# A graph network kernel whose gathers carry their milestone waits themselves

## The chip, the cores and the metric

The kernel runs on one core of a Trainium2 chip. The metric is the device time of one execution in microseconds (us). Three executions of the kernel before took 4169.53, 4178.44 and 4180.32 us; their median, 4178.44 us, is the time that the change is set against. On this core each engine has its own stream of instructions and waits for others by semaphores: TensorE (PE; its weight loads are listed as PEld), VectorE (DVE), ScalarE (ACT), GpSimd (POOL) and SyncE (SP). POOL issues nothing here but indirect DMAs, the gathers.

## What is computed

Two graph layers over 12500 nodes of 48 features and 200000 edges, sorted by destination. The first layer sends each edge's two nodes and its 32 attributes through a small network; the second adds the source node's row to 48 edge attributes. Both sum the messages by destination, add a residual and normalise each node.

```python
# layer 0
tmp = jnp.concatenate([x[dst], x[src], edge_attr_32], axis=1)
msg = jax.nn.relu(tmp @ W1 + b1) @ W2 + b2
x = _layernorm(x + segment_sum(msg, dst), axis=-1)
# layer 1
m = jax.nn.relu(x[src] + edge_attr_48)
x = _layernorm(x + (1.0 + eps[0]) * x + segment_sum(m, dst), axis=-1)
```

## The kernel before

The edges are cut into 391 groups of 512 edges, each group into four tiles of 128 edges. `x[src]` is brought by gathers: one indirect DMA (line 597 to 598, issued by the helper at line 561) fetches 128 rows of 48 floats for one tile into `edge[:, g % RING, t, 48:96]`, a ring of `RING` = 8 groups. For some groups (`PICK0_OF` in layer 0, `PICK_OF` in layer 1) the fourth tile is not gathered but picked: PE multiplies one-hot matrices `at_place` with all rows kept in `x1_parts` (`pick_rows`, line 880), DVE selects the row out of the product (lines 1104, 1113, 1118). So a group has three or four gathers.

Layer 0 runs by pairs of groups, in steps p. PE in step p (`steps0`, line 811) transposes the gathered tiles of pair p (line 805; it waits for the gathers of each group first, line 801), makes the windows of the pair (line 824, counted by the semaphore `awin`), sums the messages of pair p-3 (line 779), does the output layer of pair p-2 (line 787, counted by `msgp`) and the hidden layer of pair p-1 (line 838, counted by `pre`), then the products of the picks (line 880, a third of a step's products counted by `third`). ACT copies and activates, DVE makes one-hots, splits messages (line 1035 in layer 0, line 1037 in layer 1) and accumulates (line 1028). Layer 1 runs by single groups: DVE adds the gathered rows to the edge attributes (line 1137; it waits for the gathers first), ACT applies the relu (line 707), PE sums (line 779) and makes products (line 880).

POOL walks through the gathers in order of their groups. What it waits for is in three places:

- `gathers` (line 588) waits once per group until the group eight before it has been read (`trans` in layer 0, `sum` in layer 1), so that its place in the ring is free.
- `in_step` (line 570) spreads the up to eight gathers of a pair over PE's step: the first waits for `awin` of step g//2 - 2, the second for `msgp`, the third and fourth for `pre`, the fifth to seventh for the thirds of the products; the eighth waits for nothing.
- `in_thirds` (line 582) does so in layer 1 with the thirds of one group's products, for the first three gathers of a group.

A wait written ahead of an instruction is carried by that instruction. Each gather has a semaphore increment ahead of it, `pool.sem_inc(s_passed, 1)` (line 597), and this is the instruction that carries the waits. Nobody waits for `s_passed`. The path of the general layers (line 616), with increments of its own, is not run with these inputs.

SP's load of `x_win` for step p (line 476) waits for `awin` of step p - 2 (line 474): the same milestone for which the first gather of pair p waits.

Of the kernel before, what the change touches and what calls it, by code (L numbers as in the profile page):

```python
# [106 lines left out]
def thirds_of(products):  # L107

    n = len(products)
    return [n * k // 3 - 1 for k in (1, 2, 3)] if n >= 3 else []  # L110
# [30 lines left out]
def build(nc, x, xT, src_tiles, dst_tiles, dst_groups, e32, e48, w1, w2, b1, b2, eps, ident, iota, center, normed,  # L141
          src_rows, src_columns, places, earlier, spare, out):
    ctx = ExitStack()
    with ctx:
# [6 lines left out]
        def sem(name):  # L151
            return ctx.enter_context(nc.semaphore(name))
# [115 lines left out]
        s_passed = sem("s_passed")  # L268
# [46 lines left out]
        def wait_count(eng, s, h, per, n):  # L315
            if isinstance(h, int) and per * h + n <= 0:
                return
            eng.wait_ge(s, h * per + n)

        def peeled(eng, body, count):  # L320
            body(0)
            with eng.Fori(1, count) as i:
                body(i)
# [22 lines left out]
        def wait_for(eng, s, g):  # L346

            if g >= 0:
                eng.wait_ge(s, g + 1)
# [14 lines left out]
        def gathered(S, g):  # L364

            return TILES - 1 if g in (PICK_OF if S is S1 else PICK0_OF) else TILES
# [9 lines left out]
        def groups_of(i):  # L376
            return range(LAST + 1 if last_iteration(i) else UNROLL)
# [17 lines left out]
        def by_width(eng, general, windowed):  # L395

            eng.wait_ge(s_known, 2)
            wide_groups = eng.value_load(n_wide_i[0:1, 0:1], min_val=0, max_val=SLOTS)
            with eng.If(wide_groups > 0):
                general()  # L400
            with eng.Else():
                windowed()
# [155 lines left out]
        @block.gpsimd  # L558
        def _(pool):
            def gather(cols, rows_of, index, done):  # L560
                pool.indirect_dma_start(out=cols, out_offset=None, in_=rows_of,  # L561
                                        in_offset=bass.IndirectOffsetOnAxis(ap=index, axis=0)).then_inc(done, 16)

            def src_of(i, u, t):
                return src_all[:, (i * UNROLL + u) * TILES + t:(i * UNROLL + u) * TILES + t + 1]

            def thirds_before(products, step):
                return sum(len(thirds_of(u)) for s, u in products.items() if 0 <= s < step)

            def in_step(g, k):  # L570

                p = g // 2 - 2
                if k == 0:
                    wait_for(pool, S0["awin"], p)
                elif k == 1:
                    wait_for(pool, S0["msgp"], 2 * p - 4)
                elif k < 4:
                    wait_for(pool, S0["pre"], 2 * p - 4 + k)
                elif k < 7 and p >= 0 and thirds_of(PRODUCTS0.get(p, ())):
                    pool.wait_ge(S0["third"], thirds_before(PRODUCTS0, p) + k - 3)  # L580

            def in_thirds(g, t):

                step = g - 4
                if step >= 0 and t < 3 and thirds_of(PRODUCTS.get(step, ())):
                    pool.wait_ge(S1["third"], thirds_before(PRODUCTS, step) + t + 1)

            def gathers(S, rows_of, read, i):
                for u in groups_of(i):
                    g = i * UNROLL + u  # L590
                    wait_for(pool, S[read], g - RING)
                    for t in range(gathered(S, g)):
                        if S is S0:
                            in_step(g, g % 2 * TILES + t)
                        else:
                            in_thirds(g, t)
                        pool.sem_inc(s_passed, 1)
                        gather(edge[:, g % RING, t, D:2 * D], rows_of, src_of(i, u, t), S["rows"][g % RING])


            pool.wait_ge(s_first_src, 16)
            gathers(S0, x, "trans", 0)

            def windowed():
                def others(S, rows_of, read):
                    for i in range(1, ITERS):
                        if S is S0 and i == FIRST:
                            pool.wait_ge(s_src, 16)
                        gathers(S, rows_of, read, i)

                others(S0, x, "trans")
                pool.wait_ge(s_x1, 16 * CHUNKS)
                gathers(S1, x1_dram, "sum", 0)
                others(S1, x1_dram, "sum")

            def general_layer(G, n):
                def steps(h):
                    for u in range(2):


                        pool.wait_ge(G["idx"], h * 16 + 16)
                        wait_count(pool, G["dst"], h, 2, u + 1)
                        pool.sem_inc(s_passed, 1)
                        for t in range(TILES):
                            gather(edge[:, u, t, D:2 * D], x1_dram if n else x, idx[:, u, t:t + 1], G["rows"])
                            if n == 0:
                                gather(edge[:, u, t, 0:D], x, dst_idx[:, t:t + 1], G["rows"])
                        for t in range(TILES):


                            wait_count(pool, G["addend"], h, 2 * TILES, u * TILES + t + 1)
                            pool.sem_inc(s_passed, 1)
                            pool.indirect_dma_start(out=table[n], in_=addend[:, :], in_offset=None, compute_op=ALU.add,
                                                    out_offset=bass.IndirectOffsetOnAxis(ap=target[:, :], axis=0),
                                                    ).then_inc(G["added"], 16)

                pool.wait_ge(G["table"], 16)
                peeled(pool, steps, HALVES)

            def general():  # L640
                for u in range(UNROLL):
                    pool.wait_ge(S0["rows"][u], 16 * TILES)
                general_layer(G0, 0)
                pool.wait_ge(s_x1, 16 * CHUNKS)
                general_layer(G1, 1)

            by_width(pool, general, windowed)
# [712 lines left out]
```

## Time and profile before

| | |
|---|---|
| median of 3 runs | 4178.44 us (4169.53 to 4180.32) |
| profiled execution, its own time | 4175.66 us |
| its span, first to last instruction | 4173.9 us |
| PE busy | 3670.4 us (88%) |
| POOL busy | 2628.5 us (63%), nearly all of it in 2688 gathers |
| DVE busy | 2370.4 us (57%) |
| ACT busy | 750.7 us (18%) |
| mean granted TensorE clock | 0.883 of full speed |

The profile lists each engine's instructions with start and duration; idle time in front of one is put down to what ended it ("issue" where nothing shown ended it, "remote" where the semaphore's source could not be told). Semaphore increments, waits, register and branch instructions are not listed and do not count as busy, so POOL's `sem_inc` shows only as idle time between gathers. A gather's duration on POOL is the time in which it writes the transfer's descriptors, not that in which the data move. PE's ends are modelled. Layer 0 lasts until about 2210 us, layer 1 begins at about 2250 us.

### The profile page before, as it was taken

Reading aid. Unit: us, or ns where it says so; the run is one execution under the profiler, and the core shown is the slowest. Engines: PE = TensorE matmul, PEld = TensorE weight load, DVE = VectorE, ACT = ScalarE, POOL = GpSimd, SP = SyncE. Lnnn points to the kernel's source line nnn. Section 1 sums busy time; section 2 is a strip of 40 time slices with the busy share of each in tenths; the row PEclk is TensorE's granted clock in tenths of the full one; section 3 lists DMA queues with packets and bytes.
Section 4 is the critical chain, followed back from the end, with each engine's and each line's share of the span. In section 5 each row is a group of like instructions: output and inputs, shape, how many; then the busy total and the mean of one; then the engine's idle time right before and its main releaser. Section 6 shows DMA issues by size and latency. Waiting matters only on the chain.

```text
span 4173.9 us, 54004 instructions
## 1 busy us (share of the span) xinstructions
PE 3670.4 (88%) x18202; PEld 3023.8 (72%) x18202; DVE 2370.4 (57%) x5096; ACT 750.7 (18%) x1666; POOL 2628.5 (63%) x2692
## 2 busy tenths in 40 slices
PE   4798898888898998899998888888888889888998
PEld 3576677677777777777786777777777777777876
DVE  3344444444444444444546777776777677776766
ACT  1222222222222222222331000000000000001111
POOL 6666666666666666666664666666666666666664
PEclk7688889889898898889998899999899999998887
DMA  5222222222222222222221222222222222222221
GB/s 103 33 34 35 34 34 36 34 34 36 34 35 35 34 35 35 34 34 40 38 37 41 46 49 48 49 49 46 48 48 49 46 49 48 49 48 48 51 52 43
DMA packets 408253, 178.47 MB, mean 43 GB/s; under 512 B 279196, under 2 KB 407138, under 8 KB 407874
## 3 DMA queue, kind: packets, MB, share of 16 engines
q0 software_dynamic: 86016, 66.23, 11.6%
q1 hardware_dynamic: 319778, 108.26, 11.3%
q8 instruction: 146, 2.39, 0.2%
q14 instruction: 135, 1.11, 0.1%
q10 hardware_dynamic: 2178, 0.48, 0.1%
HBM read 169.74 MB, written 5.00 MB: 42 GB/s over the span
## 4 chain that ended last, share of the span: by engine, by line
PE 18%; DVE 17%; issue 12%; another core or an unknown queue 10%; ACT 1%; DVEq 0%; DMA 0%; POOL 0%; POOLq 0%
PE ps_h L880 5%; DVE at_place L1104 5%; DVE picked L1113 5%; PE ps_t L880 4%; PE ps_early L880 2%; PE ps_as L779 2%; DVE edgeT L1137 2%; PE ps_out L787 1%; PE ps_h L838 1%; DVE msg L1037 1%; PE ps_nodes L890 1%; ACT msg L707 1%; DVE hot L1014 1%; DVE acc L1028 1%
## 5 line engine op out<-in xcount | busy, mean ns | idle before, releaser
L561 POOL DMA_INDIRECT edge<-x,resid_sb x1430 | 1421.7, 994 | 789.1 <-issue 404.9
L561 POOL DMA_INDIRECT edge<-x_dram,resid_sb x1258 | 1206.6, 959 | 731.0 <-issue 394.8
L880 PE MATMUL ps_h<-x_parts,at_place 125*128 125x480 f32 x3080 | 799.8, 416 | 33.2 <-issue 27.3
L1104 DVE TENSOR_TENSOR at_place<-place_row,ps_out 125x1280 fp32r<-125x1280 f32 x440 | 651.4, 1481 | 236.1 <-ACT msg L687 180.6
L880 PE MATMUL ps_t<-x_parts,at_place 125*128 125x480 f32 x3040 | 757.2, 404 | 20.4 <-issue 20.1
L880 PE MATMUL ps_early<-x_parts,at_place 125*128 125x480 f32 x2680 | 733.7, 423 | 31.4 <-DVE edge L1014 18.2
L880 PEld LDWEIGHTS ps_h<-x_parts,at_place 125*128 125x128 f32 x3080 | 640.6, 211 | 150.9 <-issue 43.4
L880 PEld LDWEIGHTS ps_early<-x_parts,at_place 125*128 125x128 f32 x2680 | 526.1, 198 | 230.8 <-issue 130.5
L880 PEld LDWEIGHTS ps_t<-x_parts,at_place 125*128 125x128 f32 x3040 | 602.2, 201 | 123.1 <-issue 30.2
L779 PE MATMUL ps_as<-hot,msg 128*97 128x48 f32 x3128 | 376.4, 254 | 244.8 <-DVE msg L1037 120.6
L779 PEld LDWEIGHTS ps_as<-hot,msg 128*97 128x97 f32 x3128 | 359.3, 181 | 287.8 <-DVE msg L1037 118.6
L838 PE MATMUL ps_h<-edgeT,w_edge 128*128 128x512 f32 x782 | 488.4, 757 | 18.3 <-DMA edge<-e 14.4
L787 PE MATMUL ps_out<-w_sb,hT 128*128 128x48 f32 x3128 | 474.0, 311 | 31.0 <-issue 27.7
L787 PEld LDWEIGHTS ps_out<-w_sb,hT 128*128 128x128 f32 x3128 | 452.1, 228 | 30.3 <-issue 26.6
L1057 DVE COPY w_edge<-ps_as 48x128 f32<-48x128 f32 x391 | 112.3, 287 | 602.7 <-remote 458.4
L707 ACT ACTIVATE msg<-edgeT 128x192 fp32r<-128x192 f32 x391 | 142.6, 365 | 1566.9 <-DVE edgeT L1137 912.9
L1028 DVE TENSOR_TENSOR acc<-acc,ps_as 97x48 f32 x782 | 159.8, 204 | 443.7 <-remote 337.3
L805 PE MATMUL ps_t<-ident_sb,edge 128*128 128x128 f32 x1564 | 228.0, 286 | 99.3 <-DMA edge<-x,resid_sb 66.9
L683 ACT ACTIVATE edgeT<-ps_t 128x512 f32<-128x512 f32 x391 | 219.8, 601 | 482.5 <-PE ps_t L805 206.6
L805 PEld LDWEIGHTS ps_t<-ident_sb,edge 128*128 128x128 f32 x1564 | 194.4, 149 | 142.9 <-DMA edge<-x,resid_sb 76.1
L1118 DVE TENSOR_REDUCE edge<-picked 128x48 f32<-128x480 f32 x440 | 287.4, 653 | 15.1
L1113 DVE SCALAR_TENSOR_TENSOR picked<-iota_sb,col_rest,ps_early 128x480 f32<-128x480 f32 x134 | 143.9, 1074 | 261.2 <-remote 112.8
(77 smaller groups left out, 2140.5 us busy)
## 6 DMA issues: line engine op xcount, KB each, us to landing
edgeT<-e SPq DMA_DIRECT2D x196, 192.0 KB
place_row<-rows_dram SPq DMA_DIRECT2D x440, 62.5 KB
edge<-e SPq DMA_DIRECT2D x196, 128.0 KB
edge<-x,resid_sb POOLq DMA_INDIRECT x1430
edge<-x_dram,resid_sb POOLq DMA_INDIRECT x1258
x_win<-xT SPq DMA_DIRECT2D x391, 9.0 KB
acc<-xT SPq DMA_DIRECT2D x10, 234.4 KB
feats<-x SPq DMA_DIRECT2D x10, 234.4 KB
```

Source lines behind the costliest of these rows:

```text
L561: pool.indirect_dma_start(out=cols, out_offset=None, in_=rows_of, in_offset=bass.IndirectOffsetOnAxis(ap=index, axis=0)).then_inc(done, 16)
L683: nc.scalar.activation(edgeT[:, g % UNROLL, :], ps_t[g % 2][:, :], ACT.Copy).then_inc(S0["edgeT"], 1)
L707: nc.scalar.activation(msg[:, u, :, 0:D], pre1[:, u, :, :], ACT.Relu).then_inc(S1["high"], 1)
L779: last = nc.tensor.matmul(ps_s[g % 2], lhsT=msg[:, g % UNROLL, t, 0:SUMS], rhs=hot[:, g % UNROLL, t, :], start=(t == 0), stop=(t == TILES ...
L787: last = nc.tensor.matmul(ps_m[:, g % 2, t, :], lhsT=hT[:, g % 2, t * P:(t + 1) * P], rhs=w2_sb[:, :], start=True, stop=True)
L805: last = nc.tensor.transpose(ps_t[g % 2][:, t * P:(t + 1) * P], edge[:, g % RING, t, :], ident_sb[:, :])
L838: nc.tensor.matmul(ps_h[g % 2][:, :], lhsT=w_edge[:, g % UNROLL, :], rhs=edgeT[:, g % UNROLL, :], start=True, stop=True).then_inc(S0["pre" ...
L880: last = nc.tensor.matmul(banks[q % len(banks)], lhsT=at_place[:, q % PLACED, c, :], rhs=x1_parts[:, c, part, :], start=(c == 0 and part = ...
L1028: nc.vector.tensor_tensor(acc[0:SUMS, bass.ds(first, WIN)], acc[0:SUMS, bass.ds(first, WIN)], ps_s[g % 2], ALU.add).then_inc(S["acc"], 1)
L1104: nc.vector.tensor_tensor(at_place[:, q % PLACED, :, :], place_row[:, q % PLACED, :].unsqueeze(1).to_broadcast([NP, CHUNKS, P]), ps_places ...
L1113: nc.vector.scalar_tensor_tensor(picked[:, :, :].rearrange("p f k -> p k f"), iota_sb[:, 0:CB].unsqueeze(2).to_broadcast([P, CB, D]), col_ ...
L1118: nc.vector.tensor_reduce(edge[:, group % RING, TILES - 1, D:2 * D], picked[:, :, :], AX.X, ALU.add).then_inc(S["picked"], 1)
```

## The change

The increment ahead of each gather in `gathers` is removed. The waits are unchanged, and now stand directly ahead of the gather. The other increments of `s_passed` stay.

```diff
                         if S is S0:
                             in_step(g, g % 2 * TILES + t)
                         else:
                             in_thirds(g, t)
-                        pool.sem_inc(s_passed, 1)
                         gather(edge[:, g % RING, t, D:2 * D], rows_of, src_of(i, u, t), S["rows"][g % RING])
```

## Rows read from the trace of the kernel before

**Rows 1.** The page: busy time of each engine, and the granted clock in 40 slices

```profile
PE 3670.4 (88%) x18202; PEld 3023.8 (72%) x18202; DVE 2370.4 (57%) x5096; ACT 750.7 (18%) x1666; POOL 2628.5 (63%) x2692
...
PEclk7688889889898898889998899999899999998887
```

**Rows 2.** Busy time by stage: stretch, length, then PE, PEld, DVE, ACT, POOL, clock, DMA

```profile
1000.00:1400.00 400.00, 359.59 (x1912) 287.58 (x1909) 182.67 (x446) 104.98 (x221) 257.35 (x261) 0.89 0.22 35
...
3000.00:3400.00 400.00, 359.16 (x1672) 305.26 (x1671) 289.39 (x530) 30.34 (x83) 254.32 (x266) 0.91 0.23 48
```

**Rows 3.** Groups of instructions: line, engine, shapes, count, busy us, mean ns, idle before

```profile
L561 POOL DMA_INDIRECT edge<-x,resid_sb x1430 | 1421.7, 994 | 789.1 <-issue 404.9 <-remote 261.6 <-PE ps_h L838 56.1
L561 POOL DMA_INDIRECT edge<-x_dram,resid_sb x1258 | 1206.6, 959 | 731.0 <-issue 394.8 <-PE ps_h L880 138.6 <-PE ps_t L880 97.4
...
L1137 DVE TENSOR_TENSOR edgeT<-edge,edgeT 128x192 f32<-128x192 f32 x391 | 138.4, 354 | 1.2 <-DMA edge<-x_dram,resid_sb 1.0
...
L1014 DVE TENSOR_TENSOR hot<-iota_sb,rel 128x192 fp32r<-128x192 f32 x391 | 121.4, 352 | 0.0
```

**Rows 4.** Timeline of POOL, first gathers: start us, us, then idle before and releaser

```profile
5.21 0.95 POOL L561 DMA_INDIRECT edge<-x,resid_sb  x1 [0.31 <-issue]
6.46 0.95 POOL L561 DMA_INDIRECT edge<-x,resid_sb  x1 [0.30 <-issue]
```

**Rows 5.** Timeline, three places where `awin` releases SP's load and a gather

```profile
407.28 0.79 SPq L476 DMA_DIRECT2D x_win<-xT  x2
...
407.94 0.95 POOL L561 DMA_INDIRECT edge<-x,resid_sb  x1 [1.99 <-remote]
...
899.14 0.80 SPq L476 DMA_DIRECT2D x_win<-xT  x2
...
899.80 0.94 POOL L561 DMA_INDIRECT edge<-x,resid_sb  x1 [2.35 <-remote]
...
1022.24 0.80 SPq L476 DMA_DIRECT2D x_win<-xT  x2
...
1022.90 0.94 POOL L561 DMA_INDIRECT edge<-x,resid_sb  x1 [2.49 <-PE ps_out L787]
```

**Rows 6.** Who waited for whom, whole span: us in total, times, longest us

```profile
POOL edge L561 <- issue: 799.6, 2234, 35.4
...
PE ps_as L779 <- DVE msg L1037: 120.6, 61, 4.0
...
PEld ps_t L805 <- DMA edge<-x,resid_sb: 76.1, 38, 4.5
...
PE ps_t L805 <- DMA edge<-x,resid_sb: 66.9, 35, 4.2
PE ps_as L779 <- DVE msg L1035: 63.3, 34, 4.2
```

**Rows 7.** Line 561: who waited for the gathers in layer 1 (us, times)

```profile
  DVE edgeT L1137: 1.0, 1
```

**Rows 8.** Timeline of PE behind two waits for a gather

```profile
911.73 0.66 PE L805 MATMUL ps_t<-ident_sb,edge 128*128 128x128 f32 x4 [2.17 <-DMA edge<-x,resid_sb]
...
916.85 1.50 PE L779 MATMUL ps_as<-hot,msg 128*97 128x48 f32 x8 [4.24 <-DVE msg L1035]
...
1179.83 0.66 PE L805 MATMUL ps_t<-ident_sb,edge 128*128 128x128 f32 x4 [3.30 <-DMA edge<-x,resid_sb]
...
1180.49 1.53 PE L779 MATMUL ps_as<-hot,msg 128*97 128x48 f32 x8
```

**Rows 9.** PE around the first of these waits: stretch, length, busy, clock, DMA

```profile
900.00:908.00 8.00, 8.00 (x52) 1.00 0.41 63
...
914.00:924.00 10.00, 7.15 (x27) 0.51 0.24 37
924.00:930.00 6.00, 6.00 (x30) 0.96 0.11 16
```

## The prediction

> **What bounds the kernel now.** I read the page's busy times first. PE is at work for 88% of the span and POOL for 63% [rows 1], so PE is the engine that the time hangs on, and POOL matters only where it makes PE wait. The table by stage says the same of the middle of each layer: in 400 us of layer 0 PE is busy 359.6 us, in 400 us of layer 1 359.2 us, at a granted clock of about 0.9 [rows 2].
>
> Next, how near POOL is to its own limit. Where nothing is waited for, a gather takes 0.95 us and the next begins 0.30 us behind it: 1.25 us from start to start [rows 4]. In the middle of layer 0 POOL does 261 gathers in 400 us, one per 1.53 us; in layer 1 266, one per 1.50 us [rows 2]. So POOL would get by with some 82% of the time. Its idle time, 789.1 + 731.0 = 1520 us, is 2688 x 0.30 = 806 us of these steps between neighbours and 714 us of real waiting [rows 3].
>
> Last, who waits for the gathers. In layer 0 PE's transposes do: 76.1 us in 38 waits by the weight loads' count, 66.9 us in 35 by the matmuls' [rows 6]. In layer 1 the only reader is DVE's addition, and it waited 1.0 us in all [rows 7]. Whatever the change does to a gather by less than a microsecond is therefore worth at most those 76 us, and nothing in layer 1. The other waits of PE are for DVE's messages, 120.6 us in layer 1 and 63.3 us in layer 0 [rows 6].
>
> **What the change removes: the increments.** 2688 of them. Do they cost POOL time when it is busy? Their only room is the 0.30 us between neighbours. The row of the first gathers shows 0.30 with an increment and no wait ahead of each, and no row shows two gathers without an increment between them, so the trace bounds the part of the increment by 0 and 0.30 us. I take 0: each gather's 0.95 us would cover an increment issued ahead of time, while the one before is still writing descriptors. If I am wrong by the whole 0.30, POOL gains 2688 x 0.30 = 806 us, of which PE can use only what it waits for gathers, 76 us at the very most.
>
> **What it moves: the wait, from the increment to the gather.** This matters where POOL stands idle until the milestone comes. The trace shows such handoffs beside a second engine that waits for the same count of `awin`: SP's load of `x_win` began at 407.28, 899.14 and 1022.24 us, the gather at 407.94, 899.80 and 1022.90 us, each time 0.66 us later [rows 5]. So a gather starts at least 0.66 us behind its milestone, and a load that carries the same wait itself goes at once. If the change made the gather as quick as the load, each such handoff would be 0.66 us shorter; if the work of handing the gather to POOL starts only behind the wait, whoever carries it, it is 0. I take the upper end less a little, 0.5 us, since the engine that carries its own wait is the nearest row, and a gather surely has something left to do.
>
> The Trainium skill ("Perfetto Trace Analysis", section "DMA Instruction — SWDGE (GPSIMD)") draws it so: the sequencer decodes such a DMA, pushes it into a wait queue, is free for the next one, and the semaphore is waited for in that queue. By that rule the decoding of the gather would lie ahead of the milestone; an increment as carrier keeps it behind. The 0.66 us agree with the second half; that a gather with a wait is quicker no run here shows yet.
>
> What becomes of 0.5 us? The gathers behind the first follow at 1.25 us, so the whole chain up to the next stop moves by it, and a late group lands 0.5 us earlier. There are 38 waits, mean 2.0 us, so nearly all have 0.5 us to give: 38 x 0.5 = 19 us. Not all of it stays. Behind the wait that ended at 911.73 us PE stood still again, 4.24 us, for DVE's messages; had the transposes begun 0.5 us earlier, that second wait would have been 0.5 us longer. Behind the one that ended at 1179.83 us PE ran on without a gap, and there the gain stays [rows 8]. PE's 34 waits for line 1035 against 35 for gathers [rows 6] say that the two kinds are about equally frequent, so I keep half: **about 10 us**. In layer 1 DVE gets its rows early enough already: 0 us. Its cover is the slack that the 1.0 us show; if that is gone, a gather that comes earlier still costs nothing.
>
> Two waits on one gather (the ring's and the first milestone of a group): one of the two may need a carrier of its own, as now. It is the ring's that is old news, eight groups back, so I cost it at nothing; if the carrier held the milestone instead, the first gather of a pair would keep its 0.66 us, and the second to seventh would gain.
>
> Nothing is queued on POOL but gathers, so behind a waiting gather stand only later gathers, and they stood behind the increment before. SP and the other queues are not touched. Ring and milestones are the same counts, so no gather can start before the event that it waited for.
>
> The sum against the profiled execution: 4175.66 - 10 = 4165.7 us. That execution lies 2.8 us under the median of the runs, so **4168 us** on the scale of the median 4178.44. The case's own range is from no gain to all 19 us and the lower end of the cost, 38 x 0.66 = 25 us: 4153 to 4179.
>
> **Rivals.**
>
> Rival 1, *the handoff stays as it is*: the gather is prepared only when its wait is over. For it: nothing in the trace shows a gather that carries a wait. Against it: SP's 0.66 us lead. It gives 4178 us. The Trainium skill has a page that speaks for this one ("Vector Engine (DVE) Microarchitecture Reference", section "Instruction fetch and dispatch (NX sequencer)"): the sequencer's loop issues the semaphore wait before it reads the opcode. If issuing meant sitting it out, the change would move nothing; the page tells of DVE, not POOL.
>
> Rival 2, on the other side, *a carried wait lengthens the step between gathers*: POOL can no longer line up the next gather while one is at work, and each carrying gather costs x more than 1.25 us. Its place is the late groups of layer 0: up to eight gathers in a row end just before PE wants them, seven of them carrying a wait, so each of the 38 waits grows by 7x. It decides from the point where 7x is over the 0.5 us of the handoff, x = 0.07 us. At x = 0.15 the 38 waits are 38 x (1.05 - 0.5) = 21 us longer if no group is added to the late ones; with as many more groups falling late, 42 us: 4199 to 4220 us. The far end is x = 0.66, the whole handoff paid every time: 1.91 us for a gather where one is due every 1.53 us [rows 2], and POOL would bound the kernel: 2688 x 1.91 = 5134 us. Against it: on DVE an addition that carries a wait takes 354 ns, a comparison of the same size that carries none 352 [rows 3], so an engine does not pay for a carried wait in busy time; for POOL no row says so.
>
> Rival 3, *the clock multiplies the gain*. Ahead of the wait that ended at 911.73 us PE ran without a gap at a granted clock of 1.00, the full 2.4 GHz; then it stood idle for 2.17 and 4.24 us, and the next 10 us were granted 0.51, near the lower level of 1.2 GHz, before it was back at 0.96 [rows 8, 9]. Ten microseconds at half speed lose some 5 us of PE's work. If the shorter idle times spare a quarter of the 38 late groups this fall, 9 x 5 = 45 us come on top of 10: about 4125 us. Against it: 0.5 us off a stop of 6 us in all is little. The same coupling can turn round (one fall more), which blurs every case by some 5 to 10 us.
>
> **How the numbers follow.** Forecast, handoff shorter and half kept: 0.40, 4168 us. Rival 1: 0.25, 4178 us. Rival 2: 0.20, mostly 4199 to 4220, with a tail. Rival 3: 0.15, 4125 us. A measurement of this kernel can tell about 0.3%, 12.5 us, from no change: under 4165.9 us is faster, over 4191.0 slower. The forecast's range lies on both sides of 4165.9; I give 0.14 of its 0.40 to faster and the rest to the same. Rival 1 gives 0.22 to the same, and 0.03 to slower for the blur. Rival 2 is slower, Rival 3 faster. Faster 0.29, same 0.48, slower 0.23. The range has to hold 8 in 10: I cut the lower half of Rival 3 and the tail of Rival 2, which gives 4132 to 4218 us.
>
> **What would show it.** The handoff: at places where SP's load of line 476 and a gather are released together, the gather's start should be 0.1 to 0.2 us behind SP's instead of 0.66 (0.66 again under Rival 1). The increment's cost: neighbours still at 1.25 us; 1.0 would say that it did cost something, 1.3 or more is Rival 2. The wait of line 805 for gathers should fall from 76 to below 60 us, and the wait of line 779 for line 1035 rise by some of it. Rival 3 shows as a mean clock above 0.89. Layer 1 should keep its length within a few microseconds; if it moves by more, the gathers act on PE or DVE by a way that no wait shows, and my whole accounting by waits is wrong.

## The result, and the profile after

The changed kernel takes 4103.34 us in the median of four runs (4102.24 to 4104.37), the kernel before 4177.16 (4169.53 to 4180.32). The ratio is 0.9823, with a 95% interval of 0.9811 to 0.9835: 73.8 us faster, where 10 were forecast and the range ended at 4132. All line numbers behind 597 are one less in the changed kernel: line 805 is now 804, 779 is 778, 1137 is 1136.

The page of the kernel after: its span, the busy time of each engine and the granted clock in 40 slices. They answer to [rows 1].

```profile
span 4100.4 us, 52068 instructions
...
PE 3620.0 (88%) x18202; PEld 2975.9 (73%) x18202; DVE 2372.4 (58%) x5096; ACT 751.3 (18%) x1666; POOL 2626.6 (64%) x2692
...
PEclk7789899899898998898998989999999999999988
```

The span is 73.5 us shorter. PE has the same 18202 matmuls and is busy 50.4 us less with them (3670.4 before), its idle time is 23.1 us less; the mean granted clock rose from 0.883 to 0.898. In this pair of traces two thirds of the gain show up as faster matmuls, one third as less standing still; further down two traces of one chip split it the other way. POOL is busy as long as before.

Next the groups of the gathers (idle time before them and what ended it, as in [rows 3]) and where they begin and end (durations in ns, then first and last start in us), for the kernel after, and then the same beginnings and ends for the kernel before:

```profile
L561 POOL DMA_INDIRECT edge<-x,resid_sb x1430 | 1421.5, 994 | 747.5 <-issue 375.7 <-remote 244.0 <-PE ps_early L879 62.3
L561 POOL DMA_INDIRECT edge<-x_dram,resid_sb x1258 | 1204.9, 958 | 703.2 <-issue 347.3 <-PE ps_h L879 154.8 <-PE ps_t L879 107.3
...
L561 POOL DMA_INDIRECT edge<-x,resid_sb x1430: 938/944/1997, 3.1 to 2168.5; - x179
L561 POOL DMA_INDIRECT edge<-x_dram,resid_sb x1258: 938/944/1442, 2204.3 to 4076.6; - x180
```

```profile
L561 POOL DMA_INDIRECT edge<-x,resid_sb x1430: 941/947/2005, 3.8 to 2210.2; - x179
L561 POOL DMA_INDIRECT edge<-x_dram,resid_sb x1258: 941/947/1466, 2246.7 to 4148.0; - x180
```

Layer 0 ends 41.7 us earlier. The gathers of layer 1 take 1872.3 us from first to last instead of 1901.3: 29.0 us less in a layer in which, by [rows 7], nobody waits for them. POOL's idle time fell from 1520.1 to 1450.7 us. With its work fixed that is only the shorter span over again, so it shows where the time went on POOL and not why.

Two tables by stage, columns as in [rows 2]: layer 0 without its start, and layer 1, for the kernel after and then for the kernel before.

```profile
50.00:2168.50 2118.50, 1898.72 (x10110) 1515.76 (x10111) 952.97 (x2417) 569.89 (x1191) 1388.58 (x1396) 0.88 0.23 38
...
2204.30:4076.60 1872.30, 1662.62 (x7818) 1410.45 (x7817) 1357.59 (x2532) 161.19 (x432) 1203.98 (x1257) 0.93 0.24 49
```

```profile
50.00:2210.00 2160.00, 1921.37 (x10110) 1535.68 (x10111) 951.21 (x2416) 567.89 (x1190) 1389.25 (x1397) 0.87 0.23 37
2247.00:4148.00 1901.00, 1687.90 (x7808) 1436.55 (x7807) 1354.91 (x2526) 161.36 (x431) 1205.41 (x1258) 0.90 0.23 48
```

In layer 1 PE is busy 25.3 us less at a clock of 0.93 instead of 0.90; that is nearly the whole of its gain. In layer 0 22.7 us are busy time and 18.9 idle time (2160.00 - 1921.37 = 238.6 before, 219.8 after).

The waits of the kernel after that answer to [rows 6] (us in total, times, longest), then PE's waits ahead of its sums in layer 1 alone, for the kernel before and the one after:

```profile
PE ps_as L778 <- DVE msg L1036: 101.3, 54, 4.3
...
PE ps_t L804 <- DMA edge<-x,resid_sb: 30.9, 22, 3.7
...
PE ps_as L778 <- DVE msg L1034: 26.6, 15, 4.2
```

```profile
PE ps_as L779 <- DVE msg L1037: 115.4, 59, 4.0
PE ps_as L779 <- issue: 44.5, 46, 3.6
```

```profile
PE ps_as L778 <- DVE msg L1036: 98.5, 53, 4.3
PE ps_as L778 <- issue: 60.9, 48, 3.6
```

PE's wait for gathers fell from 66.9 us, that for layer 0's messages from 63.3. That for layer 1's messages fell from 120.6 only by name: ahead of the same sums PE also stood still where no listed event ended it ("issue"), and there the time rose by as much. With both names and 1.7 and 1.8 us for an accumulation PE stood 161.6 us ahead of layer 1's sums before and 161.2 after. In this pair the gain of layer 1 is therefore not in these waits, but in PE's busy time at a higher clock.

Last, the handoff itself. ACT's activation of line 692 (691 after) waits for the same count of `pre` as the third or fourth gather of a pair, and like SP it carries its wait itself, so places where both stood idle show how far the gather is behind. Timeline of the kernel before, then of the kernel after:

```profile
645.32 1.27 ACT L692 ACTIVATE hT<-ps_h,b_sb 128x512 f32<-128x512 f32 x2 [0.16 <-remote]
...
646.09 0.94 POOL L561 DMA_INDIRECT edge<-x,resid_sb  x1 [2.93 <-remote]
```

```profile
1911.56 1.26 ACT L691 ACTIVATE hT<-ps_h,b_sb 128x512 f32<-128x512 f32 x2 [0.84 <-remote]
...
1911.79 0.94 POOL L561 DMA_INDIRECT edge<-x,resid_sb  x1 [1.48 <-PE ps_early L879]
```

The distance is 0.77 us before and 0.23 after; it is 0.77 or 0.78 in all thirteen such places of the one trace and 0.23 or 0.24 in all five of the other. So a gather with one wait starts 0.54 us sooner. The first gather of a pair, which has the ring's wait as well as a milestone, does not. In the kernel after, SP and such a gather at a milestone of `awin`:

```profile
334.79 0.80 SPq L476 DMA_DIRECT2D x_win<-xT  x2
...
335.41 0.94 POOL L561 DMA_INDIRECT edge<-x,resid_sb  x1 [2.50 <-remote]
```

0.62 us, where [rows 5] had 0.66. Of two waits ahead of one instruction the one written first stays on it, and the later one, here the milestone, gets a carrier of its own.

### The profile page after: what moved, and what is told of

It reads as the page before. It is cut to its first block, busy times and chain, and to the rows that moved or that the text cites. A ratio compares the mean times of both kernels' runs of the same rounds, so it can differ in the third digit from the quotient of the medians.

```text
span 4100.4 us, 52068 instructions
## 1 busy us (share of the span) xinstructions
PE 3620.0 (88%) x18202; PEld 2975.9 (73%) x18202; DVE 2372.4 (58%) x5096; ACT 751.3 (18%) x1666; POOL 2626.6 (64%) x2692
## 4 chain that ended last, share of the span: by engine, by line
PE 32%; DVE 22%; issue 20%; another core or an unknown queue 17%; POOL 3%; ACT 2%; DMA 1%; DVEq 1%; SPq 0%; POOLq 0%
PE ps_early L879 8%; DVE at_place L1103 6%; DVE picked L1112 6%; PE ps_h L837 5%; PE ps_out L786 5%; PE ps_h L879 3%; POOL edge L561 3%; PE ps_as L778 3%; PE ps_t L879 3%; PE ps_t L804 3%; DVE edgeT L1136 2%; DVE hot L1013 2%; DVE acc L1027 1%; DVE msg L1036 1%
## 5 line engine op out<-in xcount | busy, mean ns | idle before, releaser
L879 PE MATMUL ps_early<-x_parts,at_place 125*128 125x480 f32 x2680 | 745.7, 426 | 68.3 <-DVE edge L1013 38.0
L879 PE MATMUL ps_h<-x_parts,at_place 125*128 125x480 f32 x3080 | 775.1, 407 | 25.2 <-issue 19.6
L879 PEld LDWEIGHTS ps_h<-x_parts,at_place 125*128 125x128 f32 x3080 | 621.8, 205 | 136.7 <-issue 34.3
L837 PE MATMUL ps_h<-edgeT,w_edge 128*128 128x512 f32 x782 | 473.6, 735 | 20.4 <-DMA edge<-e 13.9
L786 PE MATMUL ps_out<-w_sb,hT 128*128 128x48 f32 x3128 | 454.0, 302 | 24.9 <-issue 24.4
L786 PEld LDWEIGHTS ps_out<-w_sb,hT 128*128 128x128 f32 x3128 | 431.6, 219 | 27.6 <-issue 27.3
L686 ACT ACTIVATE msg<-ps_out 128x192 fp32r<-128x192 f32 x391 | 108.1, 328 | 914.3 <-remote 797.6
```

Source lines behind the costliest of these rows:

```text
L786: last = nc.tensor.matmul(ps_m[:, g % 2, t, :], lhsT=hT[:, g % 2, t * P:(t + 1) * P], rhs=w2_sb[:, :], start=True, stop=True)
L837: nc.tensor.matmul(ps_h[g % 2][:, :], lhsT=w_edge[:, g % UNROLL, :], rhs=edgeT[:, g % UNROLL, :], start=True, stop=True).then_inc(S0["pre" ...
L879: last = nc.tensor.matmul(banks[q % len(banks)], lhsT=at_place[:, q % PLACED, c, :], rhs=x1_parts[:, c, part, :], start=(c == 0 and part = ...
```

## The experiments

Every ratio is to the kernel before on the same chip, with its 95% interval; chips differ by 1%, so the times themselves compare only within a group. The letters of the theories stand for this. I: the 2688 increments themselves are what costs. H: what counts is how far a gather starts behind its milestone (the handoff). P: what counts is the way in which POOL's sequencer waits, not the distance. L: PE's semaphore updates reach the other engines late while POOL works through gathers, and that closes a loop of POOL and PE. Q and D, inside L: it is the gathers that are queued that hold the updates, or it is the length of POOL's pauses that lets them out. Many edits are counted in *stops*, places in which POOL stood idle for over 0.35 us. By the starts of the gathers the kernel before has 425: 172 in layer 0 and 122 in layer 1 at gathers with one wait, 131 at gathers with two (the first of each group).

### Is it the handoff or the increments, and in which layer?

**The increments kept, but ahead of the waits.** The gather carries the wait, and all 2688 increments are still issued.

```diff
-                    wait_for(pool, S[read], g - RING)
                     for t in range(gathered(S, g)):
+                        pool.sem_inc(s_passed, 1)
+                        if t == 0:
+                            wait_for(pool, S[read], g - RING)
                         ...
-                        pool.sem_inc(s_passed, 1)
                         gather(...)
```

> All 2688 increments are kept, but each stands ahead of the waits, so the gather carries its wait itself as in the changed kernel. Theory H (handoff: a gather that carries its wait starts sooner behind its milestone): the increments as such cost nothing, so about 4103 us, within 10 us. Theory I (increments: 2688 fewer semaphore updates leave room for PE's): the gain is gone, about 4177 us.

Measured: 4070.10 us against 4134.06, ratio 0.9838 (0.9822 to 0.9855). The ratio is that of the change within the intervals, with every increment in place: one increment a gather costs nothing that shows, its place does.

**No increments, but a carrier for the milestone.** A wait that has long been met is written ahead of the milestone, so that it stays on the gather and the milestone gets a carrier of its own.

```diff
                     for t in range(gathered(S, g)):
+                        if t > 0:
+                            pool.wait_ge(s_first_src, 16)
                         ...
-                        pool.sem_inc(s_passed, 1)
```

> No increments, but the second to fourth gather of a group get a second wait, ahead of the milestone's, on a semaphore that reached its value at the start; of two waits the later one stays on an instruction of its own ahead of the gather, so every milestone has a carrier again, only without an increment. Theory H: as the kernel before, 4165 to 4180 us, and the gathers start about 0.65 us behind SP's load again. Theory I: as the changed kernel, about 4103 us.

Measured: 4124.10 us, ratio 0.9979 (0.9964 to 0.9994). Without increments, but with the old handoff, nearly all of the gain is gone. Its timeline shows nearly the old distance, 0.74 or 0.75 us in 22 of 23 places:

```profile
847.32 1.27 ACT L693 ACTIVATE hT<-ps_h,b_sb 128x512 f32<-128x512 f32 x2 [0.84 <-remote]
...
848.06 0.95 POOL L561 DMA_INDIRECT edge<-x,resid_sb  x1 [1.72 <-remote]
```

**The change in one layer alone.** The increments stay in the other layer.

```diff
-                        pool.sem_inc(s_passed, 1)
+                        if S is S1:              # layer 0 changed; S0 here: layer 1 changed
+                            pool.sem_inc(s_passed, 1)
```

> The change in layer 0 alone. In the changed kernel the last gather of layer 0 came 42 us earlier and layer 1 took 29 us less. If each layer gains by itself: 4177 - 42 = 4135 us, with layer 1 as long as before (1901 us from first to last gather). If layer 1's gain comes from somewhere ahead of it: about 4106 us.

> The change in layer 1 alone, where nobody waited for a gather. If the 29 us of layer 1 are the change's own: 4177 - 29 = 4148 us, with a granted clock in layer 1 of 0.93 for 0.90. If they are an accident of how the layers meet: within 10 us of 4177.

Measured: layer 0 alone 4083.26 us, ratio 0.9879 (0.9862 to 0.9895), 51 us; layer 1 alone 4112.81 us, 0.9946 (0.9929 to 0.9962), 21 us. Their sum is the whole gain. Layer 1 gains by itself: it is not a gift of a layer 0 that ended in better order. The two ran on one chip, so their traces compare directly. Layer 1 from its first gather to its last, columns as in [rows 2], first with layer 0 changed, then with layer 1 changed:

```profile
2176.00:4055.00 1879.00, 1665.37 (x7817) 1421.66 (x7815) 1356.28 (x2530) 160.85 (x431) 1202.77 (x1258) 0.92 0.25 49
```

```profile
2231.00:4089.00 1858.00, 1658.35 (x7816) 1413.38 (x7815) 1355.50 (x2527) 160.81 (x431) 1200.21 (x1257) 0.92 0.25 49
```

Where layer 1 is changed it is 21 us shorter, by 7 us of PE's busy time and 14 us of its idle time. In the kernel before neither PE nor, but for 1.0 us, DVE waits for a gather in it, so the gain comes by a way on which no wait for a gather lies.

### The size of the handoff as a dose

**The kernel before once more, as a profile for its chip,** beside the next one.

> The kernel before, for a trace on the chip of the next three. No theory is at stake; time within 0.3% of the runs of before beside it.

Measured, in one execution: 4137.29 us, POOL's idle time 781.3 + 712.7 us.

**The ring's wait behind the milestone.** The milestone is written first and stays on the gather also where there are two waits.

```diff
-                    wait_for(pool, S[read], g - RING)
                     for t in range(gathered(S, g)):
                         ...
-                        pool.sem_inc(s_passed, 1)
+                        if t == 0:
+                            wait_for(pool, S[read], g - RING)
                         gather(...)
```

> The changed kernel with the two waits of a group's first gather in the other order, milestone first and ring second, so that this gather carries its milestone too and the ring's wait gets the carrier. In the changed kernel the first gathers of pairs still started 0.63 us behind SP's load. Theory H: now 0.1 to 0.25 us, and as about a third of POOL's stops are at first gathers, another 10 to 25 us: ratio to before 0.976 to 0.980. Theory P (what costs is POOL's sequencer standing in a wait ahead of the gathers, which holds up PE's updates, not the later start) says the same; if neither, ratio 0.982.

Measured: 4031.29 us (4028.75 to 4036.32) against 4136.57, ratio 0.9758 (0.9738 to 0.9777), mean clock 0.911. It beats both kernels, by 0.65% more than the change did. Its timeline at a milestone of `awin`; then PE's waits ahead of its sums behind 2150 us, in the kernel before on this chip and in this one:

```profile
1028.12 0.80 SPq L476 DMA_DIRECT2D x_win<-xT  x2
...
1028.25 0.94 POOL L561 DMA_INDIRECT edge<-x,resid_sb  x1 [1.59 <-remote]
```

```profile
PE ps_as L779 <- DVE msg L1037: 113.1, 53, 4.1
PE ps_as L779 <- issue: 62.7, 67, 4.1
```

```profile
PE ps_as L779 <- issue: 122.3, 61, 3.5
PE ps_as L779 <- DVE msg L1037: 23.7, 29, 3.5
```

The gather of a pair's start is now 0.13 us behind SP. PE stands still ahead of layer 1's sums for 146 us instead of 176; the fall from 113.1 to 23.7 by itself is mostly a change of name, since "issue" doubled. Both theories had foretold the gain, so the run does not choose between H and P.

**Seven increments in place of one,** behind the waits, so that a gather starts later behind its milestone while the step between neighbours stays at 1.25 us.

```diff
-                        pool.sem_inc(s_passed, 1)
+                        for _ in range(7):
+                            pool.sem_inc(s_passed, 1)
```

> The kernel before with seven increments ahead of each gather for one. Twelve of them made POOL itself slower (1.43 us from gather to gather, for 1.25), which mixes two causes; seven should leave the 1.25 us, and draw out only the handoff, by 6 x 0.07 = 0.4 us (0.07 us each from the twelve: 1.43 = 0.55 + 12 x 0.07). Theory H: the change took off some 0.6 us and gained 1.77%, so 0.4 us more should lose about 1.2%: ratio 1.008 to 1.016. Theory P: 0.997 to 1.003.

Measured: 4306.43 us against 4176.35, ratio 1.0315 (1.0292 to 1.0337). The direction is that of H; the size is two to four times what I expected. Timeline: the distance to ACT, and two neighbours.

```profile
808.60 1.44 ACT L693 ACTIVATE hT<-ps_h,b_sb 128x512 f32<-128x512 f32 x2 [0.20 <-remote]
...
809.85 0.94 POOL L561 DMA_INDIRECT edge<-x,resid_sb  x1 [1.08 <-remote]
```

```profile
34.08 0.95 POOL L561 DMA_INDIRECT edge<-x,resid_sb  x1 [0.30 <-issue]
35.33 0.94 POOL L561 DMA_INDIRECT edge<-x,resid_sb  x1 [0.30 <-issue]
```

The distance grew by 0.48 us, from 0.77 to 1.25, for six more increments: 0.08 us each. But that is not all that these increments did. The trace lists each of them too: most take 0.02 us, but 1009 of the 18816 take over 0.2 us, up to 1.39 us, and 145 us of this lie in POOL's pauses. POOL stood idle for over 0.35 us 636 times instead of 425, 42 times in front of a gather that waits for nothing. With one increment a gather none took over 0.2 us. So part of the 130 us is increments that were themselves held up, and this run alone does not rule out P. Here gathers also come late for both readers: DVE waited for them 292.1 us in layer 1 (1.0 before), PE 124.8 us in layer 0 (66.9 before).

The doses, side by side. *Stops* are those of the kernel before whose handoff the edit changes; *at most* is their number by the change.

| edit | handoff | stops | at most | measured | kept |
|---|---|---|---|---|---|
| the change | 0.77 to 0.23 us | 294 | -159 us | -73.8 us | 46% |
| layer 0 alone | the same | 172 | -93 us | -51 us | 55% |
| layer 1 alone | the same | 122 | -66 us | -21 us | 32% |
| ring's wait moved, on top of the change | 0.66 to 0.13 us | 131 | -69 us | -27 us | 39% |
| seven increments (not the handoff alone) | 0.77 to 1.25 us | 425 | +204 us | +130 us | 64% |

Where the handoff was shortened the time follows it at POOL's own stops, with a third to somewhat over half kept. That it does so when the handoff is lengthened is shown in direction only.

**Twelve increments, behind the waits or ahead of them.**

```diff
-                        pool.sem_inc(s_passed, 1)
+                        for _ in range(12):      # or the same lines ahead of the waits
+                            pool.sem_inc(s_passed, 1)
```

> The kernel before with twelve increments ahead of each gather for one, the first of them carrying the waits: the handoff is drawn out by eleven increments, an estimated 0.3 to 0.6 us. Theory H: slower than before, by as much again as the change gained for each 0.5 us: ratio 1.01 to 1.02. Theory P: as before, ratio 0.997 to 1.003.

> Twelve increments per gather as in the run with twelve, but ahead of the waits, so that the gather carries its wait: POOL as slow (1.43 us per gather), the handoff short. Theory H: better than the 1.058 of that run by at least the change's 1.8%, 1.01 to 1.04. If only POOL's rate counts: 1.058 again.

Measured: behind the waits 4370.36 us, ratio 1.0578 (1.0557 to 1.0600); ahead of them 4463.99 us, ratio 1.0697 (1.0668 to 1.0727). Both were misses: at most 1.02 was expected of the first, 1.01 to 1.04 of the second. H had the second 1.8% ahead of the first, and it came out 1.1% behind; why, these runs don't show. Neither tells what it was made for, since both changed the rate of POOL as well, and in both some 700 increments took over 0.2 us. Timeline of the first:

```profile
33.40 0.94 POOL L561 DMA_INDIRECT edge<-x,resid_sb  x1 [0.48 <-issue]
34.82 0.94 POOL L561 DMA_INDIRECT edge<-x,resid_sb  x1 [0.47 <-issue]
```

The step is 1.42 us instead of 1.25: POOL's sequencer has become slower than the gathers. 12 x 0.08 leave 0.46 us for the gather itself, about the 0.54 us by which the handoff shrank, so the handoff that went is most likely the sequencer's own work on the gather, which now lies ahead of the milestone. In the kernel before the increments that nothing held follow each other at 0.55 to 0.57 us, which is the same sum: one increment and one gather. At 1.42 us a gather POOL is short of time (one is due every 1.53 us in layer 0, [rows 2]), and DVE waits 521.5 us for gathers.

### Why layer 1 moves

**Layer 1 without milestones.** Its gathers wait for their place in the ring alone and so run ahead as far as they can.

```diff
                         if S is S0:
                             in_step(g, g % 2 * TILES + t)
-                        else:
-                            in_thirds(g, t)
-                        pool.sem_inc(s_passed, 1)
```

> The changed kernel with layer 1's milestones left out: its gathers wait only for their place in the ring. If an early gather is what layer 1 gains by: layer 1 shorter still, ratio 0.965 to 0.98. If the milestones are needed, to keep gathers from other work: layer 1 longer, ratio 0.985 to 1.01. If the gather's time means nothing there: 0.982.

Measured: 4292.04 us against 4136.57, ratio 1.0391 (1.0369 to 1.0413); its layer 1 takes 2076.7 us instead of 1876.6. The largest loss expected was 1.01, so this was a miss as well. Gathers that are earlier are not better as such. Where DVE stood idle for a sum, it started in the median 8.0 us after PE's sum had ended, where that was 3.4 us in the kernel before.

**Layer 1 without gathers.** The changed kernel; layer 1 computes on rows left in the ring.

```diff
-                gathers(S1, x1_dram, "sum", 0)
-                others(S1, x1_dram, "sum")
                 ...
-                    dve.wait_ge(S1["rows"][g % RING], landed(S1, g))
```

> The changed kernel without the gathers of layer 1, and without DVE's wait for them: layer 1 computes on whatever rows its ring holds. It asks why a gather that nobody waits for can cost layer 1 time. Theory L: PE's semaphore updates reach the other engines late while POOL works through gathers in a row; so without gathers DVE's accumulations no longer start microseconds behind PE's sums (in the kernel before: median 3.4 us where DVE had been idle), and layer 1 falls from 1877 us by 100 us or more: ratio under 0.96. Otherwise the lateness is PE's own, and layer 1 keeps its length: ratio 0.975 to 0.985.

Measured: 3759.25 us against 4176.35, ratio 0.9012 (0.8995 to 0.9029), the changed layer 0 included. From PE's first sum of layer 1 to its last it is 1530 us, where the changed kernel, on another chip, takes 1869. The table by stage, 400 us of its layer 1:

```profile
2800.00:3200.00 400.00, 400.00 (x2070) 348.74 (x2069) 360.18 (x663) 37.51 (x103) 0.00 (x0) 1.00 0.14 39
```

In these 400 us PE never stands still and is granted the full clock. Now the same pair of instructions in both kernels, DVE's accumulation behind PE's sum: first the kernel before, between them POOL's gathers, then the kernel without gathers in layer 1.

```profile
3031.93 0.79 PE L779 MATMUL ps_as<-hot,msg 128*97 128x48 f32 x8
...
3036.37 0.95 POOL L561 DMA_INDIRECT edge<-x_dram,resid_sb  x1 [0.30 <-issue]
...
3039.60 0.54 DVE L1028 TENSOR_TENSOR acc<-acc,ps_as 97x48 f32 x2 [5.82 <-remote]
...
3040.22 1.00 POOL L561 DMA_INDIRECT edge<-x_dram,resid_sb  x1 [2.91 <-PE ps_t L880]
...
3040.32 1.05 DVE L1113 SCALAR_TENSOR_TENSOR picked<-iota_sb,col_rest,ps_h 128x480 f32<-128x480 f32 x1
...
3040.55 0.49 PE L779 MATMUL ps_as<-hot,msg 128*97 128x48 f32 x4 [0.65 <-DVE msg L1037]
```

```profile
3009.21 0.79 PE L776 MATMUL ps_as<-hot,msg 128*97 128x48 f32 x8
...
3010.20 0.54 DVE L1025 TENSOR_TENSOR acc<-acc,ps_as 97x48 f32 x2 [1.29 <-PE ps_as L776]
```

Without gathers DVE starts 0.20 us after PE's last sum (3009.21 + 0.79 = 3010.00, then 3010.20), and so in 87 of the 89 such places of layer 1 (0.55 and 1.83 us in the other two). Before, it starts 6.9 us after it (3031.93 + 0.79 = 3032.72, then 3039.60), having stood idle for 5.82 us; POOL had been through a row of gathers that ended at 3037.32, and it too was let go by PE only now, 0.62 us behind DVE. The next instruction of PE then waited 0.65 us for DVE's message. PE's sum had long been done; what came late was the word of it. The waits of DVE for these sums between 2400 and 3600 us, the kernel before and then the one without gathers:

```profile
DVE acc L1028 <- remote: 206.0, 45, 8.8
```

```profile
DVE acc L1025 <- PE ps_as L776: 70.4, 67, 3.7
```

The trace also records the updates of the semaphores with their times, which the views above don't print; some are missing where gathers run (328 of 391 are there for layer 1's sums before, all 391 without gathers). In the example the updates of the two sums stand at 3036.58 and 3039.41 us, 4.2 and 6.7 us behind the ends of the sums. Right behind them seven updates of PE's products follow from 3039.46 to 3039.85 us, at most 0.1 us apart, though PE ends such products up to 1.3 us apart. So it is not PE that was late, but its updates, which were held and came out in a row. Without gathers every update of layer 1's sums stands 0.01 us behind the end of its sum. In the kernel before 52% of them stand over 1 us behind one; of DVE's recorded updates it is 3 of 1995, of ACT's 1 of 945.

So L holds in its first half: PE's updates are late only where gathers are at work. Whether that is how gathers act on PE without anybody waiting for them, the second half, fits all that was seen but is inferred.

The same share, of the recorded updates of layer 1's sums that stand over 1 us behind the latest end of a sum before them (a lower bound of the lateness), for the kernels of this document:

| kernel | recorded | over 1 us |
|---|---|---|
| before | 328 | 52% |
| the change | 343 | 66% |
| ring's wait moved | 329 | 61% |
| ring's wait moved, with the memset below | 340 | 80% |
| ring's wait moved, ten increments ahead, below | 293 | 19% |
| twelve increments, behind the waits / ahead | 238 / 221 | 4% / 7% |
| no gathers in layer 1 | 391 | 0% |

This also speaks against P: in the kernels in which gathers carry their waits PE's updates are not held less, but rather more often. The change does not cure the lateness; it takes 0.54 us off what is added to it.

**Is it the queue of gathers or the lack of a pause?** Two kernels, both on top of the one with the ring's wait moved. The first slows POOL's sequencer by ten increments ahead of the waits, so that fewer gathers stand ready in the queue. The second puts a short memset between the gathers of layer 1.

```diff
                     for t in range(gathered(S, g)):
+                        for _ in range(10):
+                            pool.sem_inc(s_passed, 1)
```

```diff
+                        if S is S1:
+                            nc.gpsimd.memset(pause[:, g * TILES + t:g * TILES + t + 1], 0)
```

> The kernel with swapped waits plus ten increments ahead of the waits of each gather. With 0.55 + 10 x 0.073 = 1.28 us per gather POOL's sequencer becomes as slow as POOL's gathers (1.25), so that hardly any gather stands queued behind another, while the pause between two stays about 0.33 us. Theory Q (queued gathers hold PE's updates): the late accumulations of layer 1 are gone, though the time may rise with POOL's rate. Theory D (the pause is too short): they stay late, median 3 to 4 us, as in the kernel with swapped waits. On the time: ratio 0.98 to 1.02 either way.

> The kernel with swapped waits, and in layer 1 a memset of one byte per partition on POOL ahead of each gather's waits: other work between gathers that can stay queued. Theory D: the longer time from gather to gather lets PE's updates out, and the late accumulations of layer 1 are gone, as in the runs with twelve increments. Theory Q: they stay late, median 3 us or more. Layer 1 is some 5% longer if POOL's rate falls to 1.4 us per gather.

Measured: ten increments 4435.75 us against 4163.97, ratio 1.0651 (1.0624 to 1.0678), a miss on the time (0.98 to 1.02 were expected); the memset 4075.99 us, 0.9786 (0.9770 to 0.9803). With ten increments DVE stood idle for only 10 accumulations in layer 1, and those were as late as ever (2.3 to 6.3 us, median 3.54): it now waited 528.1 us for gathers, so the engines stood at other places than before. DVE's waits therefore don't tell whether updates were still held. The recorded updates do: 19% of them over 1 us late instead of 61%. In layer 0 ACT's copy of messages started in the median 0.29 us behind PE's output layer instead of 3.18 us in the kernel with the ring's wait moved. The pause between neighbours was hardly longer: in layer 1 it was 0.30 or 0.31 us for 587 of 1257 gathers and at most 0.38 for 827. Fewer gathers queued, nearly the same pause, fewer late updates: that is what Q foretold. The memset fitted into the 0.30 us between neighbours, and the median lateness stayed at 4.07 us: other work between queued gathers doesn't let the updates out. It did not lengthen the pause, so D was not put to the test by itself; the evidence leans to Q, and a limit on the number of queued gathers by their landing was not tried. Of the miss on the time one part shows: 1056 of the increments took over 0.2 us, 163 us of it in POOL's pauses.

## Why the prediction was wrong, point by point

**The handoff: right.** A gather that carries its milestone starts 0.54 us sooner, against 0.5 forecast. The increments cost nothing (first experiment), neighbours stay at 1.25 us, and with a carrier put back nearly all of the gain is gone (second). Rival 1 falls, Rival 2 too. The section of the Trainium skill that I had cited for it ("Perfetto Trace Analysis", "DMA Instruction — SWDGE (GPSIMD)") agrees with this trace: the sequencer decodes the DMA and pushes it into the wait queue, and only there is the semaphore waited for; 0.23 us against 0.77 us with the wait on an instruction ahead. The Trainium skill's page on DVE that I cited for Rival 1 doesn't carry over to gathers on POOL.

**Which handoffs count: here it failed.** I multiplied the 0.5 us by the 38 places in which PE waited for a gather, and capped the worth of any earlier gather at those 76 us. The runs put the other number there: POOL's own stops with one wait, 294 of them. My share kept, one half, met the 46% measured, by luck: I had reasoned it from PE's next wait, and by layer and edit it ranges from 32 to 55%. 38 was the wrong count. The reason, as far as it is known, is the loop that the kernel without gathers points to. A row of gathers holds PE's updates back; DVE and ACT start late, and so does POOL's next row, since its milestone is one of those updates; to this the handoff is added, and PE's next messages come so much later. Shown are the late updates, their absence without gathers, and that the time falls with the handoff; that this is the path by which each shorter handoff reaches PE is inferred from them. In layer 1 of the kernel before and after PE's idle time hardly fell (1901.0 - 1687.9 = 213.1 us, then 1872.3 - 1662.6 = 209.7), so how its 25 us of busy time went there is not seen.

**Layer 1 at nothing: wrong, and by the test I had set.** I wrote that if it moved by more than a few microseconds, the gathers act by a way that no wait shows, and the accounting by waits is wrong. It moved by 29 us, 21 when changed alone. The trace of before had the sign: DVE released by "remote", and POOL by PE in the same moment, long after PE's sum had ended, as at 3039.60 us. I had not asked why [rows 6] names DVE's messages as PE's largest wait, while DVE is busy for 57% of the span.

**L779's wait for messages to rise: wrong.** It fell from 63.3 to 26.6 us in layer 0. I took it for the next thing in line behind a late gather. If it hangs on the same loop, as I now think, it had to shrink with it; the two runs of one chip agree, with 70.2 us where layer 0 is unchanged and 38.5 where it is changed.

**Two waits on one gather at nothing: wrong in the assignment, right in its second half.** I guessed that the ring's wait would get the carrier. It was the milestone; as I had put it for that case, the first gather kept its 0.66 us (0.62 measured). "Nothing" was also wrong: moving one line is worth 27 us more.

**The clock.** Rival 3, at 0.15, was nearest with 4125 us, and its sign came true, a mean clock above 0.89 (0.898). It had 45 us by the clock on 10 by shorter waits; measured are 50 by PE's busy time and 23 by its idle time. Its place was wrong: I tied it to the 38 late groups of layer 0, and half of the 50 us are layer 1's, where there are none. Its price was too high too: in the 10 us at 0.51 PE was busy 7.15 us [rows 9], so one fall costs 3.5 us of work and nine some 32, not 45. With PE's idle time gone, the clock is 1.00 over 400 us (kernel without gathers). How much the clock gives back for an idle microsecond is not settled. It was 2.2 us of busy time between before and after; between the kernel before and the one with the ring's wait moved, on one chip, the span is 108.6 us shorter by 62.4 us of idle and 46.2 us of busy time, which is 0.7. I had the rows for this coupling [rows 8, 9] and too few stops to apply it to.

## What to carry to other kernels

Let a gather carry the wait that is met last, and write that wait first where there are two: each further instruction or carrier between the milestone and the gather is paid at every stop of the queue's engine. Before pricing an edit by who waits for the result, compare the end of a producer with the start of its reader; where they lie microseconds apart, or the release is called "remote", the signal may be late, and the edit may act on engines that wait for nothing of its own. And add up a wait over all the names that it has, "issue" too, before calling it shorter. If a layer moves in which no listed wait should change, look there first.

## What the runs showed of the hardware that I had not expected

- While POOL works through gathers, PE's semaphore updates reach DVE, ACT and POOL late: where DVE had stood idle it started in the median 3.4 us after the end of a layer 1 sum, with up to 9.0 us of waiting, against 0.20 us in 87 of 89 places with no gathers about. The kernel whose gathers run unchecked has 8.0 us. DVE's and ACT's own updates are recorded on time. With twelve increments a gather, which slow POOL's sequencer, 4 to 7% of the updates of layer 1's sums were over 1 us late instead of 52%.
- POOL's sequencer needs about 0.5 us for a gather and 0.08 us for an increment. With one increment and with seven the commonest step is 1.25 us, with twelve 1.42 us. From seven a gather on some increments are held up themselves, for over 0.2 and up to 1.39 us.
- PE at full clock and busy for 400 us on end is possible in layer 1: without its gathers layer 1 takes 1530 us from first to last sum instead of 1869 in the changed kernel, which bounds what gathers cost there in all. Which part of a gather it is, its descriptors, its transfer or the transfer's own updates, was not separated.
